# Attention scores, VectorE's score blocks and value products on TensorE in every second step instead of every step

## The chip, the cores and the metric

One core of a Trainium2 chip runs the whole program. The metric is the device time of one execution in microseconds (us); the kernel before has a median of 1976.82 us over three runs (1975.86 to 1977.18). PE stands for TensorE, DVE for VectorE, ACT for ScalarE, POOL for GpSimd and SP for SyncE, as the profile names them.

## What is computed

x has 4096 rows of 256 features. One transformer layer is applied: attention with 16 heads of 16 features, a residual and a layer norm, then a feed-forward matmul with int8 weights, a residual and a second layer norm. The part that matters here is the attention core:

```
query = heads(ct_q @ Wu_q + b) + heads(rope(ct_q @ Wq_r + b))
key   = heads(ct_kv @ Wu_k + b) + heads(rope(x @ Wk_r + b))
value = heads(ct_kv @ Wu_v + b)
attn  = softmax(query @ key^T / scale)          # 16 heads, 4096 x 4096
out   = (attn @ value) @ Wo + bo
```

## The kernel before, in words

**Units.** The queries are cut into two halves of 2048 columns, so there are NT = 32 "heads" t (16 heads by two halves). The keys of a head are KT = 32 tiles kt of 128. A block (kt, j) is 128 keys by 512 queries, four (QB) to a tile. A score block is one fp16 matmul over 49 rows (L557). Its exponential becomes the moving operand of the value product (L600): the set of four fp32 matmuls that `values(t, kt)` issues, one to each 32-column strip of the array, runs in two passes, so it shows as eight records.

**Who makes the exponentials.** ScalarE takes most tiles: it works through `GROUPS`, 1860 groups of SLOT = 2 blocks, with one ACTIVATE of 128x1024 each (L796). 62 groups belong to head 0, 58 to each of the others. The two blocks of a group lie in different halves of the keys (tiles below and above 16) and so in different row halves of the array; only in the last two groups of a head are both in the same half. VectorE takes the tiles `BY_VECTOR` = 15, 30, 31 of a head (one tile in head 0): per block it turns scores into bits (L832), per tile it splits them (L840, L842) and evaluates a polynomial in four steps of 128x2048 (L852, L856). Those blocks come from `block(n)`, n counting up to 376.

**PSUM.** There are SLOTS = 3 places of two banks for the groups of ScalarE, so scores of group g may be written when the exponential of group g - 3 is done. Banks 6 and 7 hold VectorE's one block and the sum of the value products; they change roles from head to head.

**SBUF.** The results of ScalarE go into a ring of RING = 24 blocks, twelve groups. Before group g, ScalarE waits (L789) until the value products of the tiles of group g - 12 are done.

**The order on TensorE.** TensorE executes in order, by `attention_tensor`. At step s (there are STEPS_ALL = 1860) it waits for the exponential of group s, issues the scores of group s + 3, then a block of VectorE if `BLOCK_STEP` has one at s, one of the 16 first output projections if `PROJECT_STEP` has one (`project_first`, L604 to L610), and the value products that `VALUES[s]` plans. `value_steps` puts value products on steps with s % 3 in (0, 1), one to a step; `make_block_steps` moves VectorE's blocks to s % 3 in (2, 1). A value product of a VectorE tile is planned at least `VECTOR_LATE` = 4 steps after the last block of the next tile. `block(n)` waits until VectorE has read the block before (`b_bits`), because both use one bank; the first value product of a head waits until VectorE has read the last block of the bank that it takes over (L590); `project_first` waits for the four blocks of a tile to be read and writes into the same bank.

**The order on VectorE** is fixed in `attention_vector`: bits of a block, one polynomial step of the tile before, and hooks for other work (the copy and normalisation of a finished head at L806 to L825, the weights of the feed-forward part at L1514 to L1520, statistics and norms of the first 16 output tiles). DMA loads of the next heads are issued from SP when all groups of a head are scored (`attention_sync`).

Of the kernel before, what the change touches and what calls it, by code (L numbers as in the profile page):

```python
# [17 lines left out]
TH = HALF // 128  # L18
# [4 lines left out]
QB = HALF // CH  # L23
# [9 lines left out]
SLOTS, SLOT = 3, 2  # L33
# [4 lines left out]
def by_vector(t):  # L38

    return BY_VECTOR if t else FIRST_BY_VECTOR  # L40
# [12 lines left out]
STEPS_ALL = len(GROUPS)  # L53
# [3 lines left out]
PLACE = {(t, kt, j): (g * SLOT + k) % RING for g, (t, blocks) in enumerate(GROUPS) for k, (kt, j) in enumerate(blocks)}  # L57

LAG = 4
VALUE_PHASES = (0, 1)  # L60
BLOCK_PHASES = (2, 1)
FIRST_BLOCKS = 14
BEFORE = 3
BEHIND = 4
VECTOR_LATE = 4
URGENT = 4


def value_steps(t):

    length = HEAD_STEP[t + 1] - HEAD_STEP[t]
    steps = []
    for k in range(KT):
        s = HEAD_STEP[t] + LAG + k * length // KT
        s = max(s, steps[-1] + 1 if steps else 0)
        while s % SLOTS not in VALUE_PHASES:
            s += 1
        steps.append(min(s, STEPS_ALL))
    return steps


VALUE_STEPS = [value_steps(t) for t in range(NT)]
TURN = [steps[0] for steps in VALUE_STEPS] + [STEPS_ALL]


def make_block_steps():

    steps = []
    for t in range(NT):
        first = TURN[t] + BEHIND if t else 0  # L90
        last = TURN[t + 1] - BEFORE if t + 1 < NT else STEPS_ALL - 20
        n = FIRST_BLOCKS if t == 0 else len(BY_VECTOR) * QB
        n = min(n, QB * CYCLES - len(steps))
        for k in range(n):
            s = first + (last - first) * k // (n - 1)
            s += s % SLOTS not in BLOCK_PHASES and k < n - 1
            steps.append(s)
    return steps


BLOCK_STEP = make_block_steps()
# [5 lines left out]
def value_bank(t):  # L107

    return BANKS[(t + 1) % 2]


def block_bank(n):
    return BANKS[sum(n > of for of in COPY_AFTER) % 2]


def make_values():

    at = [[] for _ in range(STEPS_ALL + 1)]
    for t in range(NT):
        places = {kt: [HEAD_STEP[t] + n // SLOT for n, (of, j) in enumerate(HEAD_BLOCKS[t]) if of == kt] for kt in range(KT)}  # L120
        scalar = sorted((at_steps[-1], at_steps[0], kt) for kt, at_steps in places.items() if at_steps)
        vector = []
        for kt in by_vector(t):
            last = QB * TILES.index((t, kt)) + 2 * QB - 1
            vector.append((BLOCK_STEP[last] + VECTOR_LATE if last < len(BLOCK_STEP) else STEPS_ALL, kt))
        for s in VALUE_STEPS[t]:
            urgent = scalar and scalar[0][1] + RING // SLOT - 1 < s + URGENT
            if vector and not urgent and (vector[0][0] <= s or not scalar):
                at[max(s, min(vector[0][0], STEPS_ALL))].append((t, vector.pop(0)[1]))
            else:  # L130
                s = max(s, min(scalar[0][0], STEPS_ALL))
                at[s].append((t, scalar.pop(0)[2]))
    return at


VALUES = make_values()
# [12 lines left out]


PROJECT_CYCLE = next(c for c in range(CYCLES) if BLOCK_STEP[QB * c + QB - 1] >= HEAD_STEP[TH + 1])
PROJECT_STEP = {min(BLOCK_STEP[QB * (PROJECT_CYCLE + n) + QB - 1] + 3, BLOCK_STEP[QB * (PROJECT_CYCLE + n + 1)] - 1): n for n in range(TH)}
STATS_BLOCK = QB * (PROJECT_CYCLE + TH)
NORM_BLOCK = STATS_BLOCK + TH + 12

# [1 line left out]
def project_bank(n):  # L157
    return block_bank(QB * (PROJECT_CYCLE + n) + QB - 1)


OT = value_bank(0)
assert len(PROJECT_STEP) == TH and NORM_BLOCK + TH + 8 < QB * CYCLES
KR = 6 * HD
# [41 lines left out]
def build(nc, xT_d, x_d, w_d, bias_d, rows_d, tab_d, sel_d, ident_d, w8_d, out_d,  # L205
# [11 lines left out]
    with ctx:  # L217
# [3 lines left out]
        def sem(name):  # L221
            return ctx.enter_context(nc.semaphore(name))
# [101 lines left out]
        def ring(at, n=1):  # L324

            if at < RING_A:
                return arena[:, at * CH:(at + n) * CH]
            return pool_a[:, (RING_B + at - RING_A) * CH:(RING_B + at - RING_A + n) * CH]
# [31 lines left out]
        def bank(b, n=1):  # L360
            return PS[:, b * CH:(b + n) * CH]
# [23 lines left out]
        s_bo2 = sem("out_bias_made")  # L385
# [167 lines left out]
        def attention_tensor(pe, a):  # L553
            def score_block(out, par, kt, j):
                low = 64 * (kt // UPPER)
                at = kt % UPPER * 128
                return nc.tensor.matmul(out, Kst[par][low:low + HK + 1, at:at + 128],  # L557
                                        Qst[par][low:low + HK + 1, j * CH:(j + 1) * CH], start=True, stop=True)

            def scores(g):  # L560
                t, blocks = GROUPS[g]
                if g == HEAD_STEP[t]:
                    pe.wait_ge(a.stack[t % 2], STACK_INC * (t // 2 + 1))
                for k, (kt, j) in enumerate(blocks):
                    last = score_block(bank(g % SLOTS * SLOT + k), t % 2, kt, j)
                last.then_inc(a.qk, 1)

            def block(n):
                c, j = divmod(n, QB)
                t, kt = TILES[c]  # L570
                if j == 0 and kt == by_vector(t)[0]:
                    pe.wait_ge(a.stack[t % 2], STACK_INC * (t // 2 + 1))
                if j == 0 and PROJECT_CYCLE < c <= PROJECT_CYCLE + TH:

                    pe.wait_ge(p_added, c - PROJECT_CYCLE)
                if n - 1 in COPY_AFTER:

                    pe.wait_ge(a.norm, NORM0 + NSTEP * COPY_AFTER[n - 1] + 1)
                if n:
                    pe.wait_ge(b_bits, n)  # L580
                score_block(bank(block_bank(n)), t % 2, kt, j).then_inc(b_qk, 1)

            def values(t, kt):
                first, last_kt = VALUE_ORDER[KT * t][1], VALUE_ORDER[KT * t + KT - 1][1]
                if kt == first:

                    pe.wait_ge(a.vh[t % 2], 16 * (t // 2 + 1))
                    if t:

                        pe.wait_ge(b_bits, COPY_BLOCK[t - 1] + 1)  # L590
                    if t == 2:
                        pe.wait_ge(s_ones, ONES_ALL)
                vector = kt in by_vector(t)
                if vector:
                    c = TILES.index((t, kt))
                    pe.wait_ge(b_exp, c + 1)
                for j in range(QB):
                    at = None if vector else PLACE[t, kt, j]
                    moving = poly[c % 2][:, j * CH:(j + 1) * CH] if vector else ring(at)
                    last = nc.tensor.matmul(bank(value_bank(t))[32 * j:32 * j + 32, :],  # L600
                                            Vh[t % 2][:, kt, :], moving, start=kt == first, stop=kt == last_kt)
                last.then_inc(a.pv, 1)

            def project_first(n):  # L604
                if n == 0:
                    pe.wait_ge(a.heads[0], 16 * 2)
                    pe.wait_ge(a.yb, KT)

                pe.wait_ge(b_bits, QB * (PROJECT_CYCLE + n + 1))
                project_tile(n, bank(project_bank(n))[:, 0:D]).then_inc(p_proj, 1)  # L610

            bias_out()
            for g in range(SLOTS):
                scores(g)
            for s in range(STEPS_ALL + 1):
                if s < STEPS_ALL:
                    pe.wait_ge(a.exp, s + 1)
                if s + SLOTS < STEPS_ALL:
                    scores(s + SLOTS)
                for n, at in enumerate(BLOCK_STEP):  # L620
                    if at == s:
                        block(n)
                if s in PROJECT_STEP:
                    project_first(PROJECT_STEP[s])
                for t, kt in VALUES[s]:
                    values(t, kt)

        def bias_out():

            for k in range(2):  # L630
                last = nc.tensor.matmul(PS[:, OT * CH:OT * CH + D], bv_wide[:, k, :],
                                        w[:, W_O + k * D:W_O + (k + 1) * D], start=k == 0, stop=k == 1)
            last.then_inc(s_bo, 1)

        def project_tile(t, out, cs=(0, 1), starts=True, stops=True):


            for c in cs:
                last = nc.tensor.matmul(out, heads_out(t // TH, c, t % TH * 128, 128),  # L639
                                        w[:, W_O + c * D:W_O + (c + 1) * D], start=c == 0 and starts, stop=c == 1 and stops)  # L640
            return last
# [393 lines left out]
        def _(pe):  # L1035
# [89 lines left out]
            pe.wait_ge(s_sums, 1)  # L1125

            attention_tensor(pe, fast)


# [598 lines left out]
```

## Time and profile before

| | us |
|---|---|
| median of three runs | 1976.82 |
| the profiled execution, its own time | 1975.18 |
| its span, first to last instruction | 1973.3 |
| first start of the exponentials (L796) | 156.8 |
| last start of the exponentials | 1890.2 |
| ACT busy | 1815.7 (92%) |
| PE busy | 1853.5 (94%) |
| DVE busy | 1574.9 (80%) |
| granted TensorE clock, mean | 0.983 |

Time before the first exponential is the projections; the attention takes most of the span; what follows the last exponential is the second half's output projection and the feed-forward part. A line of the trace's timeline gives start, length, engine, line, operation, tiles and count; instructions of one kind that follow each other are merged, and the bracket is the idle time before them and who ended it. Starts are recorded; ends of matmuls are modelled.

### The profile page before, as it was taken

To read this page: it belongs to the slowest core of one execution; us is meant where nothing else is said; L and a number is where in the kernel's file an instruction comes from. 1 tells how busy PE (TensorE), PEld (TensorE's weight loads), DVE (VectorE), ACT (ScalarE), POOL (GpSimd) and SP (SyncE) were. 2 spreads that over 40 slices of the span, in tenths; PEclk is the share of its full clock that TensorE was granted. 3 is DMA by queue.
4 is the path that set the end of the run, shared out by engine and by line. 5 is a ranking of instruction groups with operands and counts; after the bars stand their busy time and mean duration, and the time that the engine had idled before them with its cause. 6 is when DMAs were issued, how large, how long until landed. Compare 5 with 4: busy or idle time off the path is not lost.

```text
span 1973.3 us, 31790 instructions
## 1 busy us (share of the span) xinstructions
PE 1853.5 (94%) x13009; PEld 451.6 (23%) x13009; DVE 1574.9 (80%) x1496; ACT 1815.7 (92%) x2026; POOL 157.7 (8%) x132
## 2 busy tenths in 40 slices
PE   8977999999999999999999999999999999999975
PEld 3441212121221221221222222222122112212134
DVE  3753888888888888888888788888988998888467
ACT  4447999999999999999999999999999999999955
POOL 5733500000000000000000000000000210000011
PEclk9998999999999999999999999999999999999997
DMA  5644111101101111111111001111111010111002
GB/s 182 221 141 175 25 25 25 25 17 20 22 18 25 25 25 25 25 25 25 25 36 51 16 16 25 25 25 25 25 37 34 16 19 18 25 25 25 1 24 86
DMA packets 165483, 81.48 MB, mean 41 GB/s; under 512 B 130204, under 2 KB 146716, under 8 KB 164856
## 3 DMA queue, kind: packets, MB, share of 16 engines
q1 hardware_dynamic: 164024, 78.11, 15.2%
q8 instruction: 103, 1.69, 0.4%
q10 hardware_dynamic: 1312, 1.32, 0.2%
q14 instruction: 44, 0.36, 0.1%
HBM read 48.83 MB, written 29.23 MB: 40 GB/s over the span
## 4 chain that ended last, share of the span: by engine, by line
ACT 69%; PE 13%; issue 10%; DVE 3%; DMA 2%; SPq 1%; POOL 1%; ACTq 0%; DVEq 0%; POOLq 0%
ACT arena L796 69%; PE PS L600 6%; PE PS L557 3%; PE PS L1042 2%; PE PS L639 1%; PE PS L1213 1%; DMA Qst<-parts_or_sums 1%; DMA arena<-xT_dram 1%; POOL arena L1361 1%; DVE bn L727 1%; DVE parts_or_sums L1474 0%; POOL arena L1360 0%; SPq L482 0%; DMA bias<-biases_dram 0%; POOL arena L1363 0%
## 5 line engine op out<-in xcount | busy, mean ns | idle before, releaser
L796 ACT ACTIVATE arena<-PS 128x1024 f32<-128x1024 f32 x1860 | 1712.5, 1151 | 35.2 <-PE PS L557 34.0
L600 PE MATMUL PS<-arena,Vh 128*32 128x512 f32 x8192 | 1093.6, 606 | 4.4 <-DVE arena L856 2.6
L557 PE MATMUL PS<-Qst,Kst 49*128 49x512 f16 x4096 | 712.0, 384 | 62.3 <-ACT arena L796 48.8
L856 DVE SCALAR_TENSOR_TENSOR arena<-arena 128x2048 f32<-128x2048 f32 x282 | 644.8, 2287 | 0.1
L832 DVE TENSOR_SCALAR arena<-PS 128x512 int32<-128x512 f32 x376 | 259.7, 691 | 273.1 <-PE PS L557 268.8
L557 PEld LDWEIGHTS PS<-Qst,Kst 49*128 49x128 f16 x4096 | 182.7, 93 | 1050.9 <-ACT arena L796 1002.5
L600 PEld LDWEIGHTS PS<-arena,Vh 128*32 128x32 f32 x8192 | 161.6, 108 | 337.1 <-issue 330.4
L852 DVE SCALAR_TENSOR_TENSOR arena<-arena 128x2048 f32<-128x2048 f32 x94 | 216.0, 2298 | 0.0
L840 DVE TENSOR_SCALAR arena<-arena 128x2048 int32<-128x2048 int32 x94 | 115.7, 1231 | 7.3
L842 DVE TENSOR_SCALAR arena<-arena 128x2048 int32<-128x2048 int32 x94 | 116.2, 1236 | 0.0
L1381 POOL TENSOR_SCALAR nmr<-mv 128x16 f32<-128x16 f32 x1 | 0.3, 263 | 1221.7 <-DVE mv L1527 1221.7
L1042 PE MATMUL PS<-arena,w 128*128 128x512 f32 x192 | 89.0, 612 | 9.1 <-DMA bias<-biases_dram 6.5
L1248 ACT ACTIVATE arena<-PS,bias 128x512 f32<-128x512 f32 x56 | 38.3, 686 | 40.6 <-PE PS L1042 35.0
L1042 PEld LDWEIGHTS PS<-arena,w 128*128 128x128 f32 x192 | 37.5, 197 | 57.2 <-issue 52.0
L1462 DVE TENSOR_TENSOR arena<-arena 128x512 f32<-128x512 f32 x16 | 17.4, 1088 | 40.1 <-POOL arena L1363 40.1
L769 POOL TENSOR_TENSOR arena<-arena,rows 128x256 f32<-128x256 f32 x32 | 45.3, 1453 | 37.4 <-DMA arena<-x_dram 37.4
L773 POOL TENSOR_TENSOR arena<-arena,rows 128x256 f32<-128x256 f32 x16 | 11.1, 728 | 334.5 <-ACT arena L759 334.5
L1360 POOL TENSOR_TENSOR arena<-arena 32x512 f32<-32x512 f32 x16 | 26.0, 1624 | 36.4 <-DMA arena<-arena 36.4
L1474 DVE TENSOR_TENSOR parts_or_sums<-arena,parts_or_sums 128x1024 f16<-128x1024 f32 x16 | 28.4, 1816 | 0.0
L1361 POOL TENSOR_TENSOR arena<-arena 32x512 f32<-32x512 f32 x16 | 27.6, 1726 | 0.0
L773 POOL TENSOR_TENSOR ctkv<-arena,rows 128x256 f32<-128x256 f32 x16 | 17.5, 1132 | 114.7 <-DVE arena L754 114.7
L806 DVE COPY parts_or_sums<-PS 128x512 f32<-128x512 f32 x32 | 21.9, 684 | 4.1 <-PE PS L600 4.1
(112 smaller groups left out, 493.4 us busy)
## 6 DMA issues: line engine op xcount, KB each, us to landing
Kst<-k_halves SPq DMA_DIRECT2D x64, 128.0 KB
Qst<-q_halves SPq DMA_DIRECT2D x64, 128.0 KB
Vh<-head_values SPq DMA_DIRECT2D x30, 256.0 KB, 4.4
arena<-xT_dram SPq DMA_DIRECT2D x8, 512.0 KB, 5.1
k_halves<-parts_or_sums SPq DMA_DIRECT2D x16, 256.0 KB, 2.4
k_whole<-arena SPq DMA_DIRECT2D x8, 512.0 KB, 3.4
q_halves<-parts_or_sums SPq DMA_DIRECT2D x16, 256.0 KB, 3.4
q_whole<-arena SPq DMA_DIRECT2D x8, 512.0 KB, 4.2
```

The costliest lines, as they stand in the source:

```text
L557: return nc.tensor.matmul(out, Kst[par][low:low + HK + 1, at:at + 128], Qst[par][low:low + HK + 1, j * CH:(j + 1) * CH], start=True, stop= ...
L600: last = nc.tensor.matmul(bank(value_bank(t))[32 * j:32 * j + 32, :], Vh[t % 2][:, kt, :], moving, start=kt == first, stop=kt == last_kt)
L769: nc.gpsimd.tensor_tensor(Y[:, t, :], Y[:, t, :], bo, ALU.add).then_inc(s, 1)
L796: nc.scalar.activation(ring(at, k), bank(g % SLOTS * SLOT, k), ACT.Exp, scale=EXP_SCALE).then_inc(a.exp, 1)
L832: nc.vector.tensor_scalar(bits[:, j * CH:(j + 1) * CH].bitcast(int32), bank(block_bank(n)), LOWEST, TO_BITS, ALU.max, ALU.mult).then_inc(b ...
L840: nc.vector.tensor_scalar(mantissa.bitcast(int32), bits.bitcast(int32), 0x007FFFFF, 0x3F800000, ALU.bitwise_and, ALU.bitwise_or).then_inc( ...
L842: nc.vector.tensor_scalar(power.bitcast(int32), bits.bitcast(int32), 0x7F800000, 0x40000000, ALU.bitwise_and, ALU.bitwise_xor).then_inc(b_ ...
L852: nc.vector.scalar_tensor_tensor(out=t, in0=mantissa, scalar=POLY[3], in1=mantissa, op0=ALU.add, op1=ALU.mult).then_inc(b_poly, 1)
L856: last = nc.vector.scalar_tensor_tensor(out=t, in0=t, scalar=POLY[3 - j], in1=power if j == 3 else mantissa, op0=ALU.add, op1=ALU.mult)
L1042: last = nc.tensor.matmul(bank(out_bank), l, r, start=k == 0, stop=k == len(lhsT) - 1)
L1248: nc.scalar.activation(dst[e], bank(e), ACT.Identity, bias=bs[e], scale=scales[e]).then_inc(s_ev, 1)
L1361: nc.gpsimd.tensor_tensor(a, a, tab[par][:, 0, :], ALU.mult).then_inc(s_rope, 1)
```

## The change

TensorE acts only in odd steps s. It waits for the exponential of group s (count s + 1), issues the scores of groups s + 2 and s + 3 one behind the other, then a block of VectorE, then an output projection, then the value products planned for s - 1 and s. `value_steps` rounds each step up to an odd one (two value products may share a step), block steps are rounded up to odd ones and skip steps with two value products, and projections take the odd step with the fewest value products that begins two steps after the tile's last block. `VECTOR_LATE` becomes 6. The first value product of head 0 also waits for `s_bo2` (the output bias has been read from the bank).

```diff
 LAG = 4
-VALUE_PHASES = (0, 1)
-BLOCK_PHASES = (2, 1)
 FIRST_BLOCKS = 14
 BEFORE = 3
 BEHIND = 4
-VECTOR_LATE = 4
+VECTOR_LATE = 6
 URGENT = 4
@@ value_steps(t)
     for k in range(KT):
         s = HEAD_STEP[t] + LAG + k * length // KT
-        s = max(s, steps[-1] + 1 if steps else 0)
-        while s % SLOTS not in VALUE_PHASES:
-            s += 1
-        steps.append(min(s, STEPS_ALL))
+        steps.append(min(s | 1, STEPS_ALL))
     return steps
@@
+def values_planned(s):
+    return sum(steps.count(s) for steps in VALUE_STEPS)
@@ make_block_steps()
         for k in range(n):
             s = first + (last - first) * k // (n - 1)
-            s += s % SLOTS not in BLOCK_PHASES and k < n - 1
+            s |= 1
+            while values_planned(s) > 1:
+                s += 2
             steps.append(s)
@@
-PROJECT_STEP = {min(BLOCK_STEP[QB * (PROJECT_CYCLE + n) + QB - 1] + 3, BLOCK_STEP[QB * (PROJECT_CYCLE + n + 1)] - 1): n for n in range(TH)}
+PROJECT_STEP = {min(range(BLOCK_STEP[QB * (PROJECT_CYCLE + n) + QB - 1] + 2, BLOCK_STEP[QB * (PROJECT_CYCLE + n + 1)], 2),
+                    key=values_planned): n for n in range(TH)}
@@ values(t, kt)
                     pe.wait_ge(a.vh[t % 2], 16 * (t // 2 + 1))
+                    if t == 0:
+                        pe.wait_ge(s_bo2, 1)
@@ attention_tensor
-            for s in range(STEPS_ALL + 1):
-                if s < STEPS_ALL:
-                    pe.wait_ge(a.exp, s + 1)
-                if s + SLOTS < STEPS_ALL:
-                    scores(s + SLOTS)
+            for s in range(1, STEPS_ALL + 2, 2):
+
+                pe.wait_ge(a.exp, min(s + 1, STEPS_ALL))
+                for g in range(s + 2, min(s + 4, STEPS_ALL)):
+                    scores(g)
                 for n, at in enumerate(BLOCK_STEP):
                     if at == s:
                         block(n)
                 if s in PROJECT_STEP:
                     project_first(PROJECT_STEP[s])
-                for t, kt in VALUES[s]:
-                    values(t, kt)
+                for at in VALUES[s - 1:s + 1]:
+                    for t, kt in at:
+                        values(t, kt)
```

## Rows read from the trace of the kernel before

**Rows 1.** The page: busy time of the engines, and the chain that ended last.
```profile
PE 1853.5 (94%) x13009; PEld 451.6 (23%) x13009; DVE 1574.9 (80%) x1496; ACT 1815.7 (92%) x2026; POOL 157.7 (8%) x132
...
ACT 69%; PE 13%; issue 10%; DVE 3%; DMA 2%; SPq 1%; POOL 1%; ACTq 0%; DVEq 0%; POOLq 0%
```

**Rows 2.** All exponentials: count, min/median/max ns, first and last start.
```profile
L796 ACT ACTIVATE arena<-PS x1860: 1016/1152/1497, 156.8 to 1890.2; 128x1024 f32<-128x1024 f32 x186
```

**Rows 3.** Timeline of ACT and PE around 1148 us, ACT starting from idle.
```profile
1147.78 0.60 PE L557 MATMUL PS<-Qst,Kst 49*128 49x512 f16 x3
...
1148.21 1.02 ACT L796 ACTIVATE arena<-PS 128x1024 f32<-128x1024 f32 x1 [0.23 <-PE PS L557]
...
1149.31 0.61 PE L557 MATMUL PS<-Qst,Kst 49*128 49x512 f16 x4
1149.74 8.36 ACT L796 ACTIVATE arena<-PS 128x1024 f32<-128x1024 f32 x9 [0.51 <-PE PS L557]
```

**Rows 4.** Exponentials of 540 to 1018, 1072 to 1354, head 0, head 4, head 26.
```profile
L796 ACT ACTIVATE arena<-PS x522: 1018/1158/1281, 539.3 to 1017.7; 128x1024 f32<-128x1024 f32 x174
...
L796 ACT ACTIVATE arena<-PS x291: 1016/1100/1233, 1071.2 to 1353.0; 128x1024 f32<-128x1024 f32 x146
...
L796 ACT ACTIVATE arena<-PS x62: 1018/1164/1417, 156.8 to 214.4; 128x1024 f32<-128x1024 f32 x62
...
L796 ACT ACTIVATE arena<-PS x59: 1018/1138/1232, 374.5 to 431.6; 128x1024 f32<-128x1024 f32 x59
...
L796 ACT ACTIVATE arena<-PS x59: 1018/1138/1239, 1567.3 to 1623.9; 128x1024 f32<-128x1024 f32 x59
```

**Rows 5.** Timeline of PE, 1005.6 to 1012.6 us, an undisturbed stretch.
```profile
1005.66 0.39 PE L557 MATMUL PS<-Qst,Kst 49*128 49x512 f16 x2
...
1005.98 1.07 PE L600 MATMUL PS<-arena,Vh 128*32 128x512 f32 x8
...
1006.98 0.61 PE L557 MATMUL PS<-Qst,Kst 49*128 49x512 f16 x4
...
1007.52 1.07 PE L600 MATMUL PS<-arena,Vh 128*32 128x512 f32 x8
...
1010.05 0.60 PE L557 MATMUL PS<-Qst,Kst 49*128 49x512 f16 x4
...
1011.58 0.82 PE L557 MATMUL PS<-Qst,Kst 49*128 49x512 f16 x5
...
1012.60 0.39 PE L557 MATMUL PS<-Qst,Kst 49*128 49x512 f16 x2 [0.19 <-ACT arena L796]
```

**Rows 6.** The one exponential that runs between 1011.7 and 1012.2 us.
```profile
L796 ACT ACTIVATE arena<-PS x1: 1139/1139/1139, 1011.4 to 1011.4; 128x1024 f32<-128x1024 f32 x1
```

**Rows 7.** Who waited for whom, whole span: us, times, longest.
```profile
PE PS L557 <- ACT arena L796: 48.8, 185, 0.5
...
ACT arena L796 <- PE PS L557: 34.0, 38, 13.3
```

**Rows 8.** Timeline of PE after the last scores: four sets in a row.
```profile
1890.05 3.64 PE L600 MATMUL PS<-arena,Vh 128*32 128x512 f32 x32
```

**Rows 9.** Timeline of PE around one of the 16 first projections.
```profile
1145.08 0.39 PE L557 MATMUL PS<-Qst,Kst 49*128 49x512 f16 x2
1145.40 1.13 PE L639 MATMUL PS<-w,ctkv 128*128 128x256 f32 x4
...
1146.46 0.39 PE L557 MATMUL PS<-Qst,Kst 49*128 49x512 f16 x2
```

**Rows 10.** Timeline of PE, heads 4 and 26: waits for VectorE.
```profile
394.80 1.21 PE L600 MATMUL PS<-arena,Vh 128*32 128x512 f32 x8 [2.57 <-DVE arena L856]
...
1573.48 0.39 PE L557 MATMUL PS<-Qst,Kst 49*128 49x512 f16 x2
1575.74 1.14 PE L600 MATMUL PS<-arena,Vh 128*32 128x512 f32 x8 [1.87 <-issue]
```

## The prediction

> **What bounds the kernel now.** The page shows two engines near the limit, PE at 94% and ACT at 92% of the span, and a chain that runs 69% through ACT and 13% through PE [rows 1]. That doesn't say which of them sets the pace, so I read the exponentials one stage after another. First their own pace. When ACT starts from idle, an instruction lasts 1.02 us; nine in a row last 8.36 us, so one ends every (8.36 - 1.02) / 8 = 0.9175 us [rows 3]. That is ACT's floor: 1859 periods would take 1705.6 us. From first to last start they took 1890.2 - 156.8 = 1733.4 us [rows 2]. So **27.8 us** in all are lost against the floor, and no reordering on PE can win more than that while ACT does this work.
>
> Then where they are lost. In 540 to 1018 us, 521 periods took 478.4 us where the floor is 478.0: nothing is lost, ACT is the bound and PE only feeds it. In 1072 to 1354 us, where the 16 first projections lie, 290 periods took 281.8 against 266.1: 15.7 lost, about 1.0 per projection. Head 0 loses 57.6 - 56.0 = 1.6; head 4 loses 57.1 - 53.2 = 3.9; head 26 loses 56.6 - 53.2 = 3.4 [rows 4]. Together 25.0; the other 2.8 are spread over the heads left. In head 4 a value product waits 2.57 us for VectorE's polynomial, which the feed-forward weights have made late; in head 26 one starts 2.26 us after its scores, where 0.32 is usual, behind VectorE's hooks [rows 10].
>
> PE in the undisturbed stretch does wait for ACT (48.8 us in all, in 185 pieces of at most 0.5) [rows 7]: it has a little spare time, and three score places that let it be late by more than a step without ACT noticing.
>
> **PE's prices**, start to start [rows 5]. Scores of one group and one value set: 1006.98 - 1005.66 = 1.32 us, of which 0.32 before the set and 1.00 from the set to the next scores. Scores of two groups and a set: 1.53 (1006.98 to the scores after it, as 1010.05 to 1011.58). A VectorE block adds 0.82 - 0.60 = 0.22. A set behind a set costs (3.64 - 1.06) / 3 = 0.86 instead of 1.00 [rows 8]. A projection adds 1146.46 - 1145.40 = 1.06 [rows 9].
>
> **The change, part by part.**
>
> *Fewer turns between scores and values.* I counted the plans. Before, 1023 steps hold value sets (one of them two). After, 928 odd steps hold the 1024 sets that are planned in all: 95 have two sets, three per head, 833 and the rest one. So 95 turns go. One turn is worth what two separate rounds cost more than a joint one: 2 x 1.32 - (1.53 + 0.86) = 0.25 us, 24 us of PE time in all. PE isn't the bound in most heads, so this buys spare time and no end. I cost it at 0 where ACT is at its floor; it is part of what the projection heads gain below.
>
> *The scores come later.* This is the term that decides. Before, TensorE writes group s + 3 when group s is done, and ACT still has s + 1 and s + 2 ready: two periods of cover. After, at an odd step it writes s + 2 and s + 3, and ACT has only s + 1. The cover follows from rows. From the end of exponential s, PE's first scores start after 0.06 us (1011.40 + 1.14 to 1012.60) [rows 5, 6]; scores to ACT's start take 0.43 (1147.78 to 1148.21, and 1149.31 to 1149.74); the instruction takes 1.02 [rows 3]. Sum 1.51. It is due to end two periods after s, at 1.835. So a chunk (my word for all that PE does at one odd step) may begin **0.325 us** late before ACT loses anything. A chunk takes 1.53 with one set, 1.75 with a block too: both under 1.835, PE catches up 0.30 or 0.08. A chunk with two sets takes 2.39, so the next one is 0.555 late, and ACT loses 0.555 - 0.325 = 0.23. No block is planned on these, and they lie 9 or 10 chunks apart, enough to be on time again. 95 x 0.23 = **21.9 us**.
>
> *Projections.* All 16 fall on odd steps with one set and no block: 1.53 + 1.06 = 2.59, 0.755 late, 0.43 lost each: 6.9 us in place of 15.7.
>
> *VECTOR_LATE 6.* In head 4 the set that waits 2.57 us is planned two steps, 1.8 us, later; about 0.7 us of wait is left, of which 0.325 is covered. I take 1.0 lost instead of 3.9. The other tiles wait for nothing either way.
>
> *Block steps.* Two blocks come two steps (1.8 us) apart at the closest, while VectorE frees the bank 0.4 + 0.7 us after the scores; nothing. Blocks and values are never left out or doubled, so DVE's work is as before. DMA issues are tied to whole heads and are not moved. The wait for `s_bo2` is met long before the first value set.
>
> *Head 26* has the same hook and the same wait on VectorE's last block: 3.4 kept. *Head 0*: 1.6 kept. The other heads' small losses, 2.8, I take as 1.0, since their places now have other patterns.
>
> *The tail.* After the last exponential three sets are left instead of the last two or so: 0.4 us.
>
> **Sum.** After: 21.9 + 6.9 + 1.0 + 3.4 + 1.6 + 1.0 = 35.8 us over the floor, before 27.8: +8.0, with the tail +8.4. On the profiled execution: span 1973.3 to 1981.7, time 1975.2 to 1983.6. The median of the runs lies 1.6 higher, so **1985.2 us**.
>
> Bounds. A double chunk costs nothing if the lateness is covered after all (21.9 less: 1963), and 0.555, all its lateness, if nothing is (30.8 more: 2016). Neither end fits the rows; I stay near the middle, because each part of the 0.325 is a row of this case.
>
> **A rule that speaks for the change.** The turn between value sets and scores costs time in this trace: 1.00 against 0.86 behind a set [rows 5, 8]. The Trainium skill, TensorEngine Tiling (Array Packing), Tiling Modes (Key Properties), says that a change of tiling mode drains TensorE, and by that rule alone fewer turns should pay. The trace agrees with the rule; whether it pays is the next paragraph.
>
> **The rivals.**
>
> *A. PE sets the pace, and fewer turns shorten it.* For it: PE is 94% busy and the chain passes through it. Then 95 x 0.25 = 24 us go: 1953. Against: the 540 to 1018 stretch at ACT's floor. Chance 0.05.
>
> *B. The double chunks are hidden.* If PE's late scores reach ACT before it drains, the gain in projections and head 4 stands alone: 1963. It decides if the cover is over 0.555 instead of 0.325, or if ACT has a reserve that rows of single instructions don't show; the median exponential lasts 1.15, longer than the 1.02 from idle, so a little queueing exists. Chance 0.11.
>
> *C. Half hidden.* A double costs about 0.12: 10 us less than forecast, 1975, no change that can be measured. Chance 0.14.
>
> *D. The ring.* Slower still, at one place: with values planned later, ACT waits for ring space. The tiles 8 and 24 of a head are written by its groups 32 to 35, so group 44 needs their value sets, and the later one is now in chunk 41, which has a block in some heads. That set ends 0.06 + 0.75 + 1.06 = 1.87 us after exponential 41, with 0.04 to ACT 1.91; group 44 must start by 3 x 0.9175 - 1.02 = 1.73. Up to 0.18 per head, 5.6 in all: 1991. It decides once that set ends later than 1.7; it may coincide with a double's stall and then costs nothing. Chance 0.14.
>
> The forecast keeps 0.56.
>
> **How the numbers follow.** A measurement of this kernel tells about 0.2%, 4 us, from no change. Faster by over 0.2%: A and B, 0.16. Within: C, 0.14. Slower: forecast and D, 0.70. The range leaves out A and B and takes in C, D and an error of 0.04 us per double beyond D: 1973 to 1995.
>
> **What would show it.** The line of exponentials should run about 1741 us from first to last start. In 540 to 1018, 521 periods should take some 484 us instead of 478.4. In the timeline, ACT should be idle or late (a row beginning with idle "<-PE PS L557") once after each chunk of two sets, three times a head; L557's rows should be x4 or x5, L600's x8 or x16, and x16 in 95 places. The projection stretch should lose less than 15.7, head 4 less than 3.9. I am wrong if quiet heads stay at 53.2 us (B), if ACT's waits end on L600 (D), or if the period itself moves from 0.9175.

## The result, and the profile after

The changed kernel takes **1984.28 us** (median of 6 runs, 1983.80 to 1986.56), the kernel before 1977.19 beside it (6 runs): ratio 1.0039, 95% interval 1.0029 to 1.0050. It is slower by 7.1 us; 1985.2 was forecast.

The page of the changed kernel. L801, L604, L559 and L644 are the lines that were L796, L600, L557 and L639 before [rows 1]; in the experiments the exponentials stand in lines L796 to L804, as each edit moves them.

```profile
PE 1832.6 (92%) x13009; PEld 423.5 (21%) x13009; DVE 1572.9 (79%) x1496; ACT 1821.1 (92%) x2026; POOL 156.5 (8%) x132
...
ACT 57%; PE 22%; issue 11%; DVE 5%; POOL 2%; DMA 2%; SPq 1%; ACTq 0%; DVEq 0%; POOLq 0%
```

PE is less busy than before, 1832.6 us for 1853.5, with the same matmuls: the turns that went away did save PE time. (Not all of the 20.9 us need be turns: the kernel before also ran two stretches of the attention at a lower clock, as the last section shows.) And the chain now runs more through PE, 22% for 13%. An engine with less to do holds up the other one more. So busy time didn't decide here.

All exponentials; then those of nine heads without projections (groups 410 to 932); the projection stretch (groups 990 to 1280); head 4; head 26. Count, min/median/max ns, first and last start.

```profile
L801 ACT ACTIVATE arena<-PS x1860: 1017/1087/1350, 157.8 to 1897.5; 128x1024 f32<-128x1024 f32 x186
...
L801 ACT ACTIVATE arena<-PS x523: 1017/1098/1242, 540.1 to 1025.0; 128x1024 f32<-128x1024 f32 x175
...
L801 ACT ACTIVATE arena<-PS x291: 1017/1047/1242, 1078.8 to 1357.0; 128x1024 f32<-128x1024 f32 x146
...
L801 ACT ACTIVATE arena<-PS x59: 1018/1112/1258, 378.0 to 432.4; 128x1024 f32<-128x1024 f32 x59
...
L801 ACT ACTIVATE arena<-PS x59: 1018/1063/1241, 1572.8 to 1629.0; 128x1024 f32<-128x1024 f32 x59
```

From first to last start the exponentials take 1739.7 us, before 1733.4 [rows 2]: +6.3, where +8.0 was forecast. The span grew by 9.0; the other 2.7 lie ahead of the first exponential (1.0) and behind the last (1.7). Those two parts vary by some microseconds among the profiles of this study (first start 156.8 to 161.2, rest 83.2 to 84.8), so of the 0.4 us forecast for the tail nothing can be said.

Over the floor of 0.9175 us a group (nine heads: 522 x 0.9175 = 478.9) they lose 6.0 us, 0.66 a head. The kernel before does the same stretch, groups 410 to 932, in 479.6:

```profile
L796 ACT ACTIVATE arena<-PS x523: 1018/1157/1281, 539.3 to 1018.9; 128x1024 f32<-128x1024 f32 x175
```

The projection stretch went from 15.7 us over the floor [rows 4] to 278.2 - 266.1 = 12.1, with 15 projections in it and 15 pairs of value sets (a chunk with two value sets is a pair; the 16th projection lies in head 22, behind the stretch). Head 4 loses 54.4 - 53.2 = 1.2 for 3.9, head 26 loses 56.2 - 53.2 = 3.0 for 3.4.

The mechanism, in the timeline of PE in the changed kernel:

```profile
867.28 0.82 PE L559 MATMUL PS<-Qst,Kst 49*128 49x512 f16 x5 [0.23 <-ACT arena L801]
868.03 1.06 PE L604 MATMUL PS<-arena,Vh 128*32 128x512 f32 x8
869.12 0.61 PE L559 MATMUL PS<-Qst,Kst 49*128 49x512 f16 x4
869.65 1.92 PE L604 MATMUL PS<-arena,Vh 128*32 128x512 f32 x16
871.51 0.61 PE L559 MATMUL PS<-Qst,Kst 49*128 49x512 f16 x4
872.04 1.06 PE L604 MATMUL PS<-arena,Vh 128*32 128x512 f32 x8
```

Chunks begin at 867.28 and 869.12, 1.84 apart, at ACT's pace. The one at 869.12 has two value sets (x16), and the next begins 2.39 us later, at 871.51, 0.55 late. Prices and lateness are those of the forecast.

Read by the recorded start and end of every single exponential, each of the nine heads has its losses at the same three places: 0.24 us at its group 9, 0.24 at group 27 and 0.21 at group 44. The first two are the first groups that the chunks behind the pairs at steps 5 and 23 of the head write. Group 44 is not: its scores were issued in chunk 41, ahead of the head's third pair (chunk 43). The chain of work there, in head 12 of the changed kernel (start, us, what; the view follows each step back to what released it):

```profile
846.56 2.10 ACT arena L801 x2
848.67 0.05 issue
848.71 0.82 PE PS L559 x5
849.53 1.04 PE PS L604 x8
850.58 0.02 issue
850.60 3.00 ACT arena L801 x4
```

Exponential 41 ends at 848.67, then come the scores of chunk 41 with a block, then its one value set, and group 44 starts 0.02 us behind that set, 1.93 after exponential 41 for the 1.73 at which it was due. By the plan this set is tile 24 of the head, whose place in the ring group 44 overwrites. So this is the ring wait of rival D, at the place, with the cause and nearly the size (0.18) that D gave.

### The profile page after: what moved, and what is told of

Read it like the earlier page. It is cut to its first block, busy times and chain, and to the rows that moved or that the text cites. A ratio compares the mean times of both kernels' runs of the same rounds, so it can differ in the third digit from the quotient of the medians.

```text
span 1982.3 us, 31760 instructions
## 1 busy us (share of the span) xinstructions
PE 1832.6 (92%) x13009; PEld 423.5 (21%) x13009; DVE 1572.9 (79%) x1496; ACT 1821.1 (92%) x2026; POOL 156.5 (8%) x132
## 4 chain that ended last, share of the span: by engine, by line
ACT 57%; PE 22%; issue 11%; DVE 5%; POOL 2%; DMA 2%; SPq 1%; ACTq 0%; DVEq 0%; POOLq 0%
ACT arena L801 56%; PE PS L604 11%; PE PS L559 7%; PE PS L644 1%; PE PS L1047 1%; POOL arena L1366 1%; DVE arena L861 1%; PE PS L1218 1%; DMA Qst<-parts_or_sums 1%; DMA arena<-arena 1%; POOL arena L1365 1%; DVE bn L732 1%; POOL arena L1368 0%; DVE parts_or_sums L1479 0%; SPq L484 0%
## 5 line engine op out<-in xcount | busy, mean ns | idle before, releaser
L801 ACT ACTIVATE arena<-PS 128x1024 f32<-128x1024 f32 x1860 | 1717.7, 1102 | 33.7 <-PE PS L559 22.5
L604 PE MATMUL PS<-arena,Vh 128*32 128x512 f32 x8192 | 1072.4, 604 | 2.6 <-issue 1.6
L559 PE MATMUL PS<-Qst,Kst 49*128 49x512 f16 x4096 | 653.6, 382 | 90.0 <-ACT arena L801 73.2
L559 PEld LDWEIGHTS PS<-Qst,Kst 49*128 49x128 f16 x4096 | 144.8, 94 | 964.3 <-ACT arena L801 902.2
L604 PEld LDWEIGHTS PS<-arena,Vh 128*32 128x32 f32 x8192 | 171.2, 108 | 453.6 <-issue 450.7
L1269 ACT ACTIVATE arena<-PS 128x256 f32<-128x256 f32 x32 | 10.5, 381 | 17.7 <-PE PS L1088 17.7
```

What stands on the lines that cost most here:

```text
L801: nc.scalar.activation(ring(at, k), bank(g % SLOTS * SLOT, k), ACT.Exp, scale=EXP_SCALE).then_inc(a.exp, 1)
```

## The experiments

**1. The cover given back.** TensorE waits for each group by itself, inside the same chunk.

```diff
-                pe.wait_ge(a.exp, min(s + 1, STEPS_ALL))
-                for g in range(s + 2, min(s + 4, STEPS_ALL)):
-                    scores(g)
+                for g in (s + 2, s + 3):
+                    pe.wait_ge(a.exp, min(g - 2, STEPS_ALL))
+                    if g < STEPS_ALL:
+                        scores(g)
```

> The changed kernel with its one wait per chunk split in two: TensorE waits for the exponential of group s - 1 and issues scores s + 2, then waits for group s and issues scores s + 3. Same plans, same 928 turns, same 95 chunks with two value sets; only the cover goes from one exponential period back to two. Theory (the loss is that ACT has only one scored group left): the slack of a chunk grows from 0.325 to 0.325 + 0.9175 = 1.24 us, above the 0.555 by which a pair of sets delays the next chunk and above the 0.76 of a projection. So the losses after pairs go to zero, heads without projections fall from 0.70 us over the floor to about 0.05, the projection heads to about 1, and the time falls by 23 to 26 us, to about 1960. Rival A (TensorE's own work sets the end): no work is removed, so 1984, no change. Rival (the longer time comes from the later value products and the ring): they stay where they are, so again 1984.

Measured: **1961.64 us**, ratio to the kernel before 0.9926 (0.9913 to 0.9940). The nine heads, in the same view:

```profile
L802 ACT ACTIVATE arena<-PS x523: 1018/1112/1257, 536.1 to 1015.2; 128x1024 f32<-128x1024 f32 x175
```

479.1 us: the floor, to 0.2. Work, plans and turns are those of the changed kernel; the one wait is 23 us of its time. "TensorE's work sets the end" falls. "The later value sets do" falls as the cause of the whole, but not as a part: the wait at group 44 also goes away here with the same late value sets, because the set now starts earlier in its chunk (in head 8, 0.59 us after exponential 41 has ended; with the joint wait 0.80).

**2. The pair made short.** In a chunk with two value sets the second works on fewer columns, which leaves out that part of those tiles' contribution.

```diff
-                for at in VALUES[s - 1:s + 1]:
-                    for t, kt in at:
-                        values(t, kt)
+                for k, (t, kt) in enumerate([v for at in VALUES[s - 1:s + 1] for v in at]):
+                    values(t, kt, 64 if k and s < STEPS_ALL else CH)
```

> The changed kernel in which the second value set of a chunk works on 64 of its 512 columns (94 of the 95; so those tiles' contribution to seven eighths of the queries is left out). Waits and order unchanged. Theory: the chunk then takes about 1.65 us, under 1.835, and its loss of 0.24 goes away: 94 x 0.24 = 22 us at most, a little less where a ring wait is left: 1963 to 1968. Rival A (TensorE bound): all the time taken out counts, 94 x 0.75 = 70 us: about 1914. Rival (order or turns cost, not the second set): 1984.

Measured: 1969.20 us, ratio 0.9960 (0.9945 to 0.9975), one microsecond over the expected band, and far from the 1914 at which PE's time would count in full. The other two sizes (448 and 384 in place of 64) ran later on another chip, where the kernel before took 1979.16:

> The changed kernel in which the second value set of a chunk works on 448 of its 512 columns (94 of the 95; an eighth of those tiles' contribution is left out). It takes the lateness after a pair from 0.555 to 0.555 - 0.11 = 0.45 us. Theory (cover of 0.325 us): the loss per pair falls from 0.24 to about 0.13, a head without projections from 0.70 to 0.40 to 0.43 us over the floor, the time to about 1976. If lateness had no threshold and all TensorE time counted, the head would lose 3 x 0.11 = 0.33 less too, but so it would at every further cut.

> As before with 384 of 512 columns: lateness 0.34, about the cover of 0.325. Theory: the loss per pair is gone here, and the head is at 0.20 over the floor, the same as with 64 columns; 1969 to 1971. Without a threshold the head's loss would go on falling between 384 and 64 columns by 3 x 0.54 = 1.6 us.

Measured: 1979.54 (ratio 1.0003, 0.9992 to 1.0014) and 1973.42 (0.9970, 0.9959 to 0.9981). Against the kernel before of their own call that is +0.4 and -5.7 us; the times expected, 1976 and 1970, are -1 and -7 against 1977. The nine heads with 448, 384 and 64 columns:

```profile
L800 ACT ACTIVATE arena<-PS x523: 1017/1107/1237, 540.3 to 1023.0; 128x1024 f32<-128x1024 f32 x175
```
```profile
L800 ACT ACTIVATE arena<-PS x523: 1017/1113/1243, 539.6 to 1020.8; 128x1024 f32<-128x1024 f32 x175
```
```profile
L800 ACT ACTIVATE arena<-PS x523: 1017/1167/1351, 539.5 to 1019.9; 128x1024 f32<-128x1024 f32 x175
```

| columns of the second set | 512 | 448 | 384 | 64 |
|---|---|---|---|---|
| lateness after a pair, us | 0.555 | 0.45 | 0.34 | none |
| nine heads over 478.9, per head, us | 0.66 | 0.42 | 0.26 | 0.17 |
| of this at groups 9 and 27, each | 0.24 | 0.12 | 0.02 | none |
| of this at group 44 | 0.21 | 0.21 | 0.21 | 0.21 |

The first cuts save 0.24 and 0.16 us a head; the last takes 1.6 us a head off PE and saves 0.09. So there is a threshold: what a pair costs is its lateness less 0.32 to 0.33 in all three sizes that cost anything, which is the forecast cover of 0.325. The loss at group 44 doesn't change with the pair's columns. With 64 columns it is all that is left (0.17 in the whole head, as 0.04 is won elsewhere), and the chain there, in head 8, is the same:

```profile
631.64 0.82 PE PS L559 x5
632.47 1.04 PE PS L604 x8
633.50 0.02 issue
633.53 2.66 ACT arena L800 x3
```

The third pair of a head comes just behind this stall and costs nothing that can be seen: ACT is already 0.21 us later, so the chunk behind it is late by only 0.34 against it, which the cover hides but for 0.02. No run moves the value set of chunk 41 by itself.

**3. More pairs, with the joint and with the split wait.** The same work, three value sets a head moved one chunk on.

```diff
         steps.append(min(s | 1, STEPS_ALL))
+    for k in range(4, KT - 4, 9):
+        steps[k] = steps[k + 1]
     return steps
```

> The changed kernel with three value sets per head moved one chunk on, so that 160 chunks hold two sets, 67 hold none, instead of 95 and 2; the same work with 64 fewer turns between scores and values. Theory: each pair more costs about 0.24 us of ACT's time, a little more where two lie close: 65 x 0.24 = 16 to 20 us, 2000 to 2005. Rival A (turns on TensorE set the time): 64 turns less are 64 x 0.25 = 16 us faster, 1968.

> Both edits at once: 160 pairs and the split wait. Theory: with 1.24 us of cover a pair costs nothing, however many there are; only the projection heads lose more because pairs and projections add up. About 5 us over the kernel with the split wait alone: 1965, while the same plan with the joint wait is at 2000 or more. Rival (pairs cost by themselves, whatever the wait): 16 to 20 us over the split wait alone.

Measured: 2006.45 (ratio 1.0151, 1.0135 to 1.0166) and 1966.68 (0.9949, 0.9934 to 0.9964). With the joint wait 65 pairs more and 65 turns fewer (64 by the expectation) cost 22 us, slightly over the band; with the split wait 5.0. The two above the band are explained by group 44: a head of the changed kernel has three pairs of which two cost, a head here has five pairs away from group 44, and each costs 0.235 us (at groups 9, 17, 27, 33 and 49); 31 x 3 x 0.235 = 21.9. In the nine heads:

```profile
L803 ACT ACTIVATE arena<-PS x523: 1017/1059/1233, 545.3 to 1036.2; 128x1024 f32<-128x1024 f32 x175
```
```profile
L804 ACT ACTIVATE arena<-PS x523: 1015/1059/1220, 535.5 to 1014.9; 128x1024 f32<-128x1024 f32 x175
```

490.9 against 479.4 us. In heads without projections a pair costs only where the cover is one period. The 5.0 us are mostly in the stretch of the projections, which loses 10.7 us here and 6.3 with the split wait alone: there a pair and a projection add up, as expected.

**4. Only the cover taken away, from the kernel before.**

```diff
-                if s + SLOTS < STEPS_ALL:
-                    scores(s + SLOTS)
+                if SLOTS <= s + 2 < STEPS_ALL:
+                    scores(s + 2)
```

> The kernel before, acting in every step and with its own plans, but at step s it issues the scores of group s + 2 instead of s + 3, so that ACT has one scored group left while TensorE works, as in the changed kernel; one of the three places is always unused. Theory (cover is what counts): a step with a set takes 1.32 us against a period of 0.9175 and two such steps follow each other, so TensorE is up to 0.8 us late against 0.325 of cover, many times in each head: about 5 us more per head, 1977 + 161 = 2138, within 30. Rival A (turns or TensorE's work set the time): same work, same turns, 1977.

Measured: 2141.80 us, ratio 1.0833 (1.0813 to 1.0852), 4 us from the expected 2138. Who waited for whom, whole span:

```profile
PE PS L557 <- ACT arena L796: 166.2, 391, 1.3
...
ACT arena L796 <- PE PS L557: 138.4, 378, 12.8
```

Against 48.8 and 34.0 before [rows 7], both engines now wait for each other, which is what a buffer too small looks like in this view. Of ACT's 378 waits some 340 are new.

**5. VECTOR_LATE alone, both ways.**

```diff
-VECTOR_LATE = 6
+VECTOR_LATE = 4
```

> The changed kernel with VECTOR_LATE back at 4. Theory: nothing changes in 30 heads; in head 4 the value set of a VectorE tile again waits for the polynomial, and about 2 us of that reach ACT, in head 26 about 1: 1.5 to 3.5 us more than the changed kernel, 1986 to 1988. If the other 30 heads move too, the later value sets played a part of their own.

> The kernel before with VECTOR_LATE = 6 alone. Theory: head 4 loses 1.5 to 2.5 us less, the rest stays: 1975, 0 to 2.5 us under the kernel before, hardly told from it by the medians but seen in head 4 of the trace.

Measured: the changed kernel with 4 takes 1991.30 (ratio 1.0067, 1.0052 to 1.0083), the kernel before with 6 takes 1974.69 (0.9986, 0.9977 to 0.9995). Head 4 in either:

```profile
L801 ACT ACTIVATE arena<-PS x59: 1016/1093/1242, 382.1 to 439.7; 128x1024 f32<-128x1024 f32 x59
```
```profile
L796 ACT ACTIVATE arena<-PS x59: 1018/1141/1231, 378.0 to 432.0; 128x1024 f32<-128x1024 f32 x59
```

57.6 us with 4, against 54.4 in the changed kernel, and 54.0 with 6 in the kernel before, against 56.9: 2.9 saved in the head, where at most 2.5 was expected. The nine quiet heads of both stay as they were. Head 26 of the kernel with 4 also got slower, 58.7 us for 56.2. I had expected 1.5 to 3.5 us for the first and got 7.0 by the medians, of which heads 4 and 26 hold 5.7 in the trace and head 0 holds 0.7. What makes it that much in heads 4 and 26 stands in the last section.

**6. The projections made short**, 32 of 256 columns, the rest of those tiles left out.

```diff
-                project_tile(n, bank(project_bank(n))[:, 0:D]).then_inc(p_proj, 1)
+                project_tile(n, bank(project_bank(n))[:, 0:32], n=32).then_inc(p_proj, 1)
```

> The changed kernel in which the 16 first projections compute 32 of their 256 output columns (the other columns of those tiles are left out). A projection then takes some 0.2 to 0.3 us instead of 1.06, so its chunk stays under 1.835 us. Theory: the projection heads lose what the others lose, 0.70 us instead of 2.43; with the 5 heads and the part of a sixth that is about 9 us: 1975. Rival (the projection heads lose by VectorE's adds or by the waits for its bits): they stay near 2.4, 1984.

Measured: 1978.72 us, ratio 0.9999 (0.9988 to 1.0011) beside 1979.16 for the kernel before, so 5.6 us under the changed kernel by the medians, and 8 if each is taken against the kernel before beside it; 9 were expected. The stretch of the projections:

```profile
L801 ACT ACTIVATE arena<-PS x291: 1018/1075/1242, 1079.1 to 1350.6; 128x1024 f32<-128x1024 f32 x146
```

271.5 us for 278.2: 6.7 of its 12.1 us over the floor were the projections' length on PE; VectorE's adds and the waits for bits are still there and don't make it. 5.4 are left. Ten pairs at 0.24 and five waits at group 44 at 0.21 are 3.4 of it; and the last projection of each of the five heads still costs 0.36 us, 1.8 in all, for a reason given in the next section.

**7. The version that beats both.** The split wait, and VectorE's two long reductions moved away from head 26.

```diff
-            hooks.update({NORM_BLOCK + TH + 4 * q: lambda q=q: first_largest(q) for q in range(2)})
+            hooks.update({NORM_BLOCK + TH + 5 + 4 * q: lambda q=q: first_largest(q) for q in range(2)})
```

> The split wait, and VectorE's two reductions over the first 16 tiles (2.3 us each) moved five blocks later, away from the block whose bits head 26 waits for. Theory: head 26 loses 2.4 us less and nothing else moves: 1959.5, 2 us under the split wait alone and 17 to 18 under the kernel before. Rival (head 26 waits for something else): 1961.6.

Measured: **1958.48 us** (4 runs, 1957.99 to 1959.36), ratio to the kernel before 0.9905 (0.9890 to 0.9921). Head 26 with the split wait alone, and with the reductions moved:

```profile
L802 ACT ACTIVATE arena<-PS x59: 1019/1072/1258, 1553.8 to 1609.6; 128x1024 f32<-128x1024 f32 x59
```
```profile
L802 ACT ACTIVATE arena<-PS x59: 1018/1119/1244, 1554.2 to 1607.5; 128x1024 f32<-128x1024 f32 x59
```

55.8 and 53.3 us, the floor being 53.2: 2.5 less, where 2.4 was expected.

## Why the prediction was right, point by point

**ACT's floor.** Right: 0.9175 us a group held in every run; the split wait runs nine heads at 479.1 us against 478.9.

**PE's prices.** Right: a chunk with a pair takes 2.39 us in the trace after, the next is 0.55 late. By the plans value sets now stand in 929 places instead of 1023 (834 with one set, 94 pairs, and one pair behind the last exponential; the forecast's 928 and 95 are off by one). 94 turns less did go with 21 us less of PE's busy time, and bought nothing.

**Cover of 0.325 us, 0.23 lost for each of 95 pairs.** Right in mechanism and in the price of a pair: 0.24, and the cover comes out at 0.32 to 0.33 (experiment 2). Wrong in the count: of a head's three pairs two cost, and the third stands behind the ring wait at group 44. 2 x 0.24 + 0.21 is nearly 3 x 0.23, so the sum came out close, 20.5 us in 31 heads for 21.9, from other parts than the forecast's. That is in part luck: the two stalls happen to be of one size.

**Projections, 0.43 each, 6.9 in all.** A part of the sum was too small. Eleven of the sixteen lose 0.44, but the last one in each of five heads loses 0.86. Timelines of ACT and PE at one of either kind:

```profile
1171.64 1.94 ACT L801 ACTIVATE arena<-PS 128x1024 f32<-128x1024 f32 x2 [0.33 <-PE PS L559]
...
1189.24 3.77 ACT L801 ACTIVATE arena<-PS 128x1024 f32<-128x1024 f32 x4 [0.75 <-PE PS L559]
```
```profile
1168.62 0.61 PE L559 MATMUL PS<-Qst,Kst 49*128 49x512 f16 x4
...
1185.79 0.82 PE L559 MATMUL PS<-Qst,Kst 49*128 49x512 f16 x4
1186.54 1.13 PE L644 MATMUL PS<-w,ctkv 128*128 128x256 f32 x4
...
1188.60 0.82 PE L559 MATMUL PS<-Qst,Kst 49*128 49x512 f16 x5
```

The same four score matmuls take 0.61 us at 1168.62 and 0.82 at 1185.79. The latter hold a group at a head's end, whose two blocks lie in the same row half of the array, and take 0.21 more. The next chunk starts with the second such group: ACT starts it 0.64 us after its scores (1188.60 to 1189.24), where 0.43 is usual. Together 0.42 is added where the projection has already used up the cover. The short projections of experiment 6 bear this out: by themselves they are inside the cover, and only those at a head's end still cost, 0.36. My step "a chunk takes 1.53" left this out, though the kernel's text gave it: 5 x 0.42 = 2.1 us, and 9.1 instead of 6.9.

The stretch of 1072 to 1354 us that the forecast reads for "the 16 first projections" holds 15 of them; its sum for 16 doesn't depend on that.

**VECTOR_LATE.** Right in the wait, too high in its cost. The forecast's 1.0 comes on top of the head's pairs; head 4 loses 1.2 in all, 0.5 more than a quiet head. The 0.7 us of wait forecast is there as 0.73:

```profile
398.40 1.07 PE L604 MATMUL PS<-arena,Vh 128*32 128x512 f32 x8 [0.73 <-DVE arena L861]
```

**The others.** Head 26 lost 3.0 in all, 2.4 more than a quiet head, for 3.4 on top of its pairs. Head 0 lost 1.8 for 1.6, and the small losses of the other heads, 1.0 in the forecast, are gone. By the trace the sum was 35.8 - 34.1 = 1.7 too high: 1.4 on the pairs, 0.5 on head 4, 1.0 on head 26 and 1.0 on the small losses, less the 2.2 that the projections lacked and 0.15 in head 0. So the total is closer than its terms, which erred both ways.

**Rival A** (PE sets the pace) fell in experiments 1, 2 and 3; **B and C** (pairs hidden) by the nine heads; the reserve that B asked for doesn't exist beyond the 0.325. **D** (the ring) is there, in every quiet head, with 0.21 us at group 44. It adds nothing to the whole, because it takes the place of what the third pair would have cost, as D itself allowed. Its sign, ACT's waits ending on the value sets, doesn't show in the list of waits, since ACT is idle only 0.11 us there; it shows in the chain.

**What I had said would show it** was half wrong. A pair leaves no idle row of ACT: between 861.52 and 878 all its instructions are one row, x18, without a bracket. Each instruction is recorded as started before the one ahead of it has ended (min 1.02, median 1.10, max 1.24 us long, one every 0.92), and a stall of 0.24 eats that overlap and leaves 0.13 us of idle time, which the rows merge. Only the projections' stalls are long enough to show as 0.33 and 0.75. One has to read first and last start of a counted stretch, not the idle time. And the total of a head doesn't tell which wait made it: that took the single exponentials and the chain.

One row was read for more than it says: the 48.8 us that PE waits for ACT [rows 7] are of the whole span, not of the undisturbed stretch; in 500 to 1000 us they are 13.9. Nothing in the sum rests on it.

## What to carry to other kernels

When an engine is fed through a few places, grouping the feeder's work saves the feeder time and takes cover from the fed one; compute how late a group may begin (periods of cover, less wake-up, work and hand-over, all rows of a timeline) and compare it with the longest group. If the grouping is worth having, keep the single waits inside it: here the same grouped order is 1.1% faster than with the joint wait. Against the kernel before it is 0.7% faster, of which VECTOR_LATE alone gives 0.1 (experiment 5); with VectorE's two reductions moved as well, 1%. The two reductions were not moved in the kernel before, so what they are worth there isn't shown. Judge a saturated engine by the start of its first and last instruction in a counted stretch against its period.

## What the runs showed that I had not expected

After a long wait TensorE's granted clock fell, from 2.4 to 1.2 GHz for some microseconds. In the kernel before, after the waits of 2.57 us in head 4 and 2.26 us in head 26 [rows 10], the clock was 0.60 and 0.58 in the stretch behind them: most of it at 1.2 GHz. The changed kernel has no such drop in the whole attention part (granted clock 1.00 from 170 to 1890 us). The windows' columns are PE, PEld, DVE, ACT, POOL busy, PEclk, DMA share, GB/s; first the kernel before, then the changed one behind its waits in the same heads (0.73 us in head 4, 1.59 in head 26).

```profile
395.00:398.00 3.00, 3.00 (x19) 0.63 (x15) 2.97 (x4) 1.35 (x2) 0.00 (x0) 0.60 0.00 0
1576.00:1580.00 4.00, 4.00 (x22) 0.44 (x14) 3.90 (x5) 1.94 (x2) 4.00 (x4) 0.58 0.14 55
```
```profile
398.00:401.00 3.00, 2.60 (x22) 0.50 (x24) 2.86 (x4) 2.58 (x3) 0.00 (x0) 1.00 0.00 0
1584.00:1588.00 4.00, 3.77 (x31) 0.75 (x29) 3.76 (x7) 4.00 (x6) 4.00 (x6) 1.00 0.12 34
```

In experiment 5 the wait of head 4 is back, and a value set soon behind it takes 1.94 us instead of 1.06:

```profile
402.50 1.06 PE L604 MATMUL PS<-arena,Vh 128*32 128x512 f32 x8 [2.77 <-DVE arena L861]
403.50 0.85 PE L559 MATMUL PS<-Qst,Kst 49*128 49x512 f16 x5
404.28 1.94 PE L604 MATMUL PS<-arena,Vh 128*32 128x512 f32 x8
```

The 4 us from 404 on have a granted clock of 0.57, and so have 4 us in head 26, behind a wait of 2.10 us that the changed kernel doesn't have there:

```profile
404.00:408.00 4.00, 4.00 (x23) 0.54 (x20) 3.80 (x3) 2.89 (x3) 0.00 (x0) 0.57 0.00 0
1602.00:1606.00 4.00, 4.00 (x23) 0.59 (x17) 3.59 (x4) 1.94 (x2) 0.00 (x0) 0.57 0.00 0
```

So such a wait is paid twice: what reaches ACT of the wait itself, and the slow matmuls after it. In head 4 of that run ACT loses 2.2 us at the wait and 1.8 in the next groups. This is why VECTOR_LATE is worth more in experiment 5 than the wait's length. In the kernel before with VECTOR_LATE at 6 the wait of head 4 is 0.25 us and the clock stays at 1.00 there. The Trainium skill, TensorE: Matmul & The Clock Gate, Part 1, describes a clock that is halved when the array has been idle. This trace agrees that it is halved behind a wait: 0.57 to 0.60 behind waits of 1.87 to 2.77 us, 1.00 behind waits of 0.73 and 1.59. But in the run of experiment 4 it also stayed at 1.00 behind a wait of 1.96 us in head 4, so the length of the wait alone doesn't settle it. How the level follows in detail from what PE did in these stretches was not tried further.
